# Four-layer cross-attention on one core: layer 2's score products, queries and keys moved between steps, and the mask count cut into eight pieces

## The chip, the core and the metric

The kernel runs on one core of one Trainium2 chip. The metric is device time in microseconds, the median of the runs shown. The core's engines run side by side and wait for each other on semaphores: TensorE (PE) multiplies, VectorE (DVE) does elementwise work and reductions, ScalarE (ACT) does activations and copies out of PSUM, GpSimd (POOL) does elementwise work in SBUF, and SyncE (SP) issues the DMAs. Each engine executes its own instructions in the order written.

## What is computed

Eight batches of 100 rows of width 128 go through four layers with 16 heads of 8. Layers 0, 1 and 3 attend to 1444 rows of context, layer 2 to the first 100 rows of the context under a causal mask, followed by a feed-forward with a GELU.

```
x = L0(x, ctx)        # rmsnorm; 1444 keys; output projection; xn + out
x = L1(x, ctx, mask)  # 1444 keys, score masked to -inf where mask is True; projection; layer norm
x = L2(x, ctx)        # keys = ctx[:, :100] under a causal mask; layer norm;
                      #   gelu(att_h @ W1.T + b1) @ W2.T + b2 + att_h
x = L3(x, ctx)        # 1444 keys; layer norm
```

The mask of layer 1 is an input of booleans and is False everywhere; the kernel counts its non-zero bytes and branches on the count.

## The kernel before

**Units and stages.** A unit is one of the layers 0, 1, 3 for one batch: 24 units. The program is a software pipeline over stages, n = -3 to 24. In stage n, unit n runs its exponentials (`exp`), unit n+1 finishes its running maximum (`top`), unit n+2 projects queries and keys (`prep`), unit n+3 is loaded (`load`), unit n-1 is finished (`post`). Layer 2 of a batch has no stage of its own: its attention (`att2`) rides in the stage four ahead of the batch's layer-3 unit, which makes stages 12 to 19, and its layer norm and feed-forward (`ff2`) in the next, stages 13 to 20.

**Steps.** A stage has 48 steps, `NSTEP = NCH * T`: 12 chunks of 120 or 121 keys by four groups of four heads. In each step PE computes a score tile into one of the three `sexp` banks (`exp_product`), and another, 13 steps ahead (`LEAD`), into one of four `ring` banks (`max_product`). ACT takes exp of the `sexp` tile into `probs` (L1030, `exps`), DVE folds the `ring` tile into the running maximum `mx` (L1246, `maximum`). PE can run three steps ahead of ACT: `exp_product` of step j waits until the exp of step j-3 is done. In every fourth step PE multiplies four steps of `probs` with the values (`values`, L778). `exp_product`, `max_product` and most other products show up at the line of the helper that issues them, L608.

**Where the other work goes.** Three tables of step numbers say behind which step each other piece of work stands, on PE, ACT and DVE alike: `AT` for layers 0, 1 and 3 (xT the transposed input, q the queries, k0 to k2 the keys, v0 to v2 the values, mk0 to mk2 the mask, OT and wo the output projection of `post`, mt0, mt1 and mn the maxima), `AT2` for layer 2's attention (kqv its keys, queries and values; s0 to s3 the scores of four heads each; e0 to e3 their exp on ACT; pt0 to pt3 their transposition), `AT2_FF` for its feed-forward (scale the second half of the layer norm on DVE; at the transposition of its result `att2`; h the hidden layer, whose four GELUs on ACT need another activation table; w2 the second product).

**Who waits for what, near the change.** For a score tile s*t* of layer 2, DVE adds the causal mask (L1327, `causal2`) in the same step and takes the negated maximum (L1333, `maximum2`) in the next, POOL adds it (L525, `less_maximum`), ACT takes exp at e*t* (L1062), PE transposes at pt*t* (L835), ACT copies (L1065). The scores need `kbd2` from POOL (L517, `spread2`). For the queries, PE multiplies at step q, ACT copies to `qh` (L1018), DVE makes `qs` (L1233) in the same step, and POOL spreads it into `qx` (L534). POOL's order in a stage is fixed: context halves (L497, L499), `spread2`, the layer norm's root of `ff2` (L505), `spread`, the root of a layer-1 `post`, four `less_maximum`. The root of `ff2` is what DVE's scale (L1276) waits for.

**Ring banks.** Four `ring` banks serve all products but `sexp` and `acc`. `place` assigns each product a bank in advance, the one planned to be free first, from the step tables and the hold times in `HOLD`; a product waits until the bank's last reader is done.

**The mask count.** In stage -1 (`FLAG_STAGE - 1`), behind v2, ACT adds up all mask bytes, 9025 a partition, in one activation (L1103); at the end of stage 0 PE sums over partitions (L908), ACT writes the flag (L1109), and PE reads it before stage 6.

## Time and profile before

| | us |
|---|---|
| median of 3 runs | 1051.69 (1050.79 to 1053.68) |
| the profiled execution | 1052.03 |
| its span, first to last instruction | 1050.2 |
| PE busy in the span | 947.4 (90%) |
| DVE busy | 839.8 (80%) |
| ACT busy | 717.6 (68%) |
| POOL busy | 372.3 (35%) |

Busy time is the union of an engine's instructions; the rest of the span it waits. TensorE's clock has two levels, 2.4 and 1.2 GHz, and the granted clock is the mean in parts of the higher: 0.958 over the span. At the lower level the same products are busy for about twice as long, so PE's busy time holds both. Stages are told apart by the first `sexp` product of each: stage 0 begins at 76.0 us in the trace, stage 12 at 511.9, stage 20 at 913.4.

### The profile page before, as it was taken

To read this page: it belongs to the slowest core of one execution; us is meant where nothing else is said; L and a number is where in the kernel's file an instruction comes from. 1 tells how busy PE (TensorE), PEld (TensorE's weight loads), DVE (VectorE), ACT (ScalarE), POOL (GpSimd) and SP (SyncE) were. 2 spreads that over 40 slices of the span, in tenths; PEclk is the share of its full clock that TensorE was granted. 3 is DMA by queue.
4 is the path that set the end of the run, shared out by engine and by line. 5 is a ranking of instruction groups with operands and counts; after the bars stand their busy time and mean duration, and the time that the engine had idled before them with its cause. 6 is when DMAs were issued, how large, how long until landed. Compare 5 with 4: busy or idle time off the path is not lost.

```text
span 1050.2 us, 43883 instructions
## 1 busy us (share of the span) xinstructions
PE 947.4 (90%) x18826; PEld 570.9 (54%) x18826; DVE 839.8 (80%) x1804; ACT 717.6 (68%) x1621; POOL 372.3 (35%) x404
## 2 busy tenths in 40 slices
PE   1889999999989999999998979898979898989996
PEld 1346556656656665666564545555645464555552
DVE  7888988889788888889987777777878787869851
ACT  1147777777767777777776676667666676767786
POOL 3835345444323312332543434334343434212100
PEclk9669999999999999999999999999989898999999
DMA  8422313222232233233313121212121211212100
GB/s 225 110 62 72 83 50 88 78 69 60 78 95 69 89 95 104 66 93 96 96 52 86 35 82 38 68 38 69 43 62 44 69 51 61 71 36 66 52 4 6
DMA packets 63641, 73.75 MB, mean 70 GB/s; under 512 B 8130, under 2 KB 59114, under 8 KB 63318
## 3 DMA queue, kind: packets, MB, share of 16 engines
q1 hardware_dynamic: 63446, 70.92, 24.3%
q8 instruction: 150, 2.46, 1.0%
q14 instruction: 45, 0.37, 0.1%
HBM read 50.35 MB, written 18.15 MB: 65 GB/s over the span
## 4 chain that ended last, share of the span: by engine, by line
PE 66%; DVE 20%; ACT 5%; issue 4%; POOL 3%; DMA 1%; SPq 1%; POOLq 0%; ACTq 0%; DVEq 0%
PE ring L608 25%; PE sexp L608 15%; PE acc L778 15%; DVE mx L1246 7%; PE ring L651 6%; DVE mneg L1252 3%; DVE mx L1244 3%; POOL kbd L517 2%; ACT probs L1030 2%; PE ring L835 1%; PE ring L628 1%; DVE kp L1223 1%; PE ring L789 1%; DMA rows<-in_rows 1%; PE ring L734 1%
## 5 line engine op out<-in xcount | busy, mean ns | idle before, releaser
L1246 DVE TENSOR_TENSOR mx<-ring,mx 120x400 f16<-120x400 f32 (+1 forms) x1056 | 564.8, 566 | 114.6 <-PE ring L608 111.7
L1030 ACT ACTIVATE probs<-sexp 120x400 f32<-120x400 f32 (+1 forms) x1152 | 529.9, 509 | 139.2 <-PE sexp L608 134.6
L608 PE MATMUL ring<-qx,krep 96*32 96x400 f16 (+2 forms) x4608 | 418.2, 348 | 30.7 <-DVE mx L1246 8.1
L608 PE MATMUL sexp<-qx,krep 97*32 97x400 f16 (+2 forms) x4608 | 410.9, 340 | 8.4 <-ACT probs L1030 4.2
L778 PE MATMUL acc<-probs,vx 120*18 120x200 f32 (+1 forms) x4608 | 254.6, 336 | 1.0 <-ACT probs L1030 0.7
L608 PEld LDWEIGHTS ring<-qx,krep 96*32 96x32 f16 (+2 forms) x4608 | 133.8, 98 | 130.4 <-DVE mx L1246 42.7
L608 PEld LDWEIGHTS sexp<-qx,krep 97*32 97x32 f16 (+2 forms) x4608 | 133.4, 97 | 94.3 <-ACT probs L1030 28.4
L778 PEld LDWEIGHTS acc<-probs,vx 120*18 120x18 f32 (+1 forms) x4608 | 133.3, 99 | 65.9 <-issue 5.4
L534 POOL TENSOR_TENSOR qx<-qs,headmask 96x400 f16<-96x400 f16 x96 | 78.8, 849 | 150.0 <-DVE qs L1233 150.0
L497 POOL CAST ct<-ctf 128x480 f16<-128x480 f32 (+1 forms) x69 | 40.4, 585 | 135.1 <-PE ring L651 75.0
L608 PE MATMUL ring<-ct,wk 128*32 128x480 f16 (+1 forms) x864 | 65.4, 389 | 20.7 <-DVE mx L1246 20.0
L499 POOL TENSOR_TENSOR ct<-ctf,ct 128x480 f16<-128x480 f32 (+1 forms) x69 | 76.3, 1105 | 5.5
L651 PEld LDWEIGHTS ring<-wv,ct 128*120 128x120 f16 (+1 forms) x864 | 56.4, 139 | 27.5 <-issue 13.7
L651 PE MATMUL ring<-wv,ct 128*120 128x128 f16 (+1 forms) x864 | 66.4, 229 | 2.3 <-DVE kp L1223 1.1
L1244 DVE CAST mx<-ring 121x400 f16<-121x400 f32 x96 | 53.0, 567 | 14.1 <-PE ring L608 14.1
L1000 ACT COPY vx<-ring 120x512 f32<-120x512 f32 (+1 forms) x72 | 42.7, 593 | 28.3 <-PE ring L651 26.9
L990 ACT ACTIVATE kp<-ring,cols 128x480 f16<-128x480 f32 (+1 forms) x48 | 31.7, 661 | 42.3 <-PE ring L608 42.3
L1252 DVE TENSOR_REDUCE mneg<-ring 100x8 f16<-100x968 f16 x48 | 55.5, 1158 | 1.2 <-PE ring L734 1.2
L505 POOL TENSOR_TENSOR rstd<-vare,half 100x1 f32<-100x1 f32 x24 | 13.3, 553 | 116.9 <-DVE vare L1268 116.9
L608 PEld LDWEIGHTS ring<-ct,wk 128*32 128x32 f16 x864 | 27.6, 100 | 37.0 <-issue 25.7
L517 POOL TENSOR_TENSOR kbd<-kq,heads 128x1600 f16<-128x1600 f16 x16 | 45.8, 2880 | 0.6
L1233 DVE SCALAR_TENSOR_TENSOR qs<-qh,headmask,ring 96x400 f16<-96x400 f16 x24 | 15.0, 627 | 36.3 <-ACT qh L1018 36.3
(137 smaller groups left out, 865.0 us busy)
## 6 DMA issues: line engine op xcount, KB each, us to landing
krep<-kept SPq DMA_DIRECT2D x144, 120.0 KB, 2.8
ctf<-in_ctxT SPq DMA_DIRECT2D x16, 722.0 KB
kept<-kp SPq DMA_DIRECT2D x48, 240.0 KB, 3.0
krep<-kept SPq DMA_DIRECT2D x72, 121.0 KB, 2.6
kept<-kp SPq DMA_DIRECT2D x24, 242.0 KB, 2.7
nat<-in_ctx SPq DMA_DIRECT2D x8, 720.0 KB
maskexp<-maskmax SPq DMA_DIRECT2D x8, 281.2 KB, 3.4
anymask<-in_mask SPq DMA_DIRECT2D x1, 1128.1 KB, 10.2
```

The source lines that it names most:

```text
L497: pool.tensor_copy(ct[:, u.par, 0, c0:c0 + n], ctf[:, c0:c0 + n]).then_inc(sem["ct_high"], 1)
L499: pool.tensor_tensor(ct[:, u.par, 1, c0:c0 + n], ctf[:, c0:c0 + n], ct[:, u.par, 0, c0:c0 + n], ALU.subtract).then_inc(sem["ct_low"], 1)
L517: last = pool.tensor_tensor(kbd2[:, i, :, :], kq16[:, i, 0, :].unsqueeze(1).broadcast_to([128, H, S]), heads16[:, :].unsqueeze(2).broadcas ...
L534: last = pool.tensor_tensor(qx[0:PARTS, u.third, t, :, :], qs[:, t, :].unsqueeze(1).broadcast_to([PARTS, HT, S]), headmask16[:, :].unsquee ...
L608: last = run(out[g:g + m], w[:, g:g + m], x, **flags)
L651: last = pe.matmul(ps[0:r, D * i:D * i + D], ct[:, u.par, p, c0:c0 + r], wv16[:, w, u.L, :], start=(j == 0), stop=(j == 2))
L778: last = pe.matmul(acc[32 * q:32 * q + VW, 2 * S * side:2 * S * side + 2 * S], vx[0:r, u.par, PAIRS * c + 2 * t + p, :], probs[0:r, j % PR ...
L1000: act.copy(vx[0:r, u.par, a0:a1, :].rearrange("p a (f e) -> p a f e", f=2)[:, :, :, 0:DH], bank(f"v{g}", u)[0:r, 0:2 * DH * (a1 - a0)].rea ...
L1030: act.activation(probs[0:r, j % PR, :], sexp[j % SR][0:r, 0:QW], ACT.Exp).then_inc(sem["probs_ready"], 1)
L1244: op = dve.tensor_copy(dst, src)
L1246: op = dve.tensor_tensor(dst, src, dst, ALU.max)
L1252: dve.tensor_reduce(mneg[:, 8 * i:8 * i + 8], bank(f"mt{i}", u)[0:S, :].bitcast(F16).rearrange("s (h n) -> s h n", h=8)[:, :, 0:chunk(0)[1 ...
```

## The change

Three things change.

**Step tables.** In every stage xT goes from step 18 to 13 and q from 20 to 16; k1 from 22 to 24, v0 from 24 to 25, v1 from 27 to 28, k2 from 30 to 31, mk0 to mk2 one step later each. In layer 2's attention the scores go from steps 23, 25, 26, 28 to 20, 21, 22, 23, their exp from 29, 31, 32, 34 to 26, 27, 29, 30, their transposition from 32, 34, 35, 38 to 27, 29, 30, 32, and the last three pieces two steps earlier. In the feed-forward, scale and at go one step later (13 and 17), h stays at 19, and w2 goes from 27 to 34.

**Mask count.** Eight activations of 1129 bytes a partition (the last of 1122) in stage 0, behind steps 4, 9, ..., 39, instead of one of 9025 in stage -1.

**Flag.** PE sums eight columns instead of one, and ACT adds these up in one more activation, on which its own copy waits.

```diff
-AT = {"ct0": 0, "ct1": 3, "ct2": 6, "O": 7, "k0": 10, "OT": 12, "wo": 15, "xT": 18, "q": 20, "k1": 22, "v0": 24,
-      "mk0": 25, "v1": 27, "mk1": 28, "k2": 30, "mk2": 31, "v2": 33, "power": 25, "scale": 32, "mt0": 36, "mt1": 37, "mn": 41}
+AT = {"ct0": 0, "ct1": 3, "ct2": 6, "O": 7, "k0": 10, "OT": 12, "xT": 13, "wo": 15, "q": 16, "k1": 24, "v0": 25,
+      "mk0": 26, "v1": 28, "mk1": 29, "k2": 31, "mk2": 32, "v2": 33, "power": 25, "scale": 32, "mt0": 36, "mt1": 37, "mn": 41}
...
-AT2_FF = {"out": 0, "scale": 12, "at": 16, "h": 19, "w2": 27}
+AT2_FF = {"out": 0, "scale": 13, "at": 17, "h": 19, "w2": 34}
...
-        maskcount = sb("maskcount", [128, 1])
+        maskcount = sb("maskcount", [128, 8])
+        masksum = sb("masksum", [1, 9])
...
-                pe.matmul(ps[0:1, 0:1], maskcount[:, :], ones[:, :], start=True, stop=True
+                pe.matmul(ps[0:1, 0:8], ones[:, :], maskcount[:, :], start=True, stop=True
...
-                    if n == FLAG_STAGE - 1 and j == AT["v2"] + 1:
+                    if n == FLAG_STAGE and j % 5 == 4 and j < 40:
                         act.wait_ge(sem["mask_in_all"], 16)
-                        act.activation(anymask[:, :], anymask[:, :], ACT.Copy, accum_out=maskcount[:, :]
+                        piece = anymask[:, j // 5 * 1129:min(j // 5 * 1129 + 1129, B * S * KEYS // 128)]
+                        act.activation(piece, piece, ACT.Copy, accum_out=maskcount[:, j // 5:j // 5 + 1]
                                        ).then_inc(sem["mask_counted"], 1)
...
-                        act.copy(maskflag[:, :], bank("flag", None)[0:1, 0:1]).then_inc(sem["flag_ready"], 1)
+                        act.activation(masksum[:, 0:8], bank("flag", None)[0:1, 0:8], ACT.Copy, accum_out=masksum[:, 8:9]
+                                       ).then_inc(sem["flag_summed"], 1)
+                        act.wait_ge(sem["flag_summed"], 1)
+                        act.copy(maskflag[:, :], masksum[:, 8:9]).then_inc(sem["flag_ready"], 1)
```

How PE's instructions stand behind the hidden layer (`aT2,w1`, step 19) in stage 14, before; steps 20 to 22, the queries behind step 20 and the keys k1 behind step 22:

```order
L608 MATMUL ring1<-aT2,w1 32x100 x16
L608 MATMUL sexp2<-qx,krep 32x400 x4
L608 MATMUL ring0<-qx,krep 32x400 x4
L608 MATMUL ring2<-which16,bq16 32x400 x3
L608 MATMUL ring2<-xT,wq 32x100 x12
L608 MATMUL sexp0<-qx,krep 32x400 x4
L608 MATMUL ring3<-qx,krep 32x400 x4
L608 MATMUL sexp1<-qx,krep 32x400 x4
L608 MATMUL ring0<-qx,krep 32x400 x4
L778 MATMUL acc<-probs,vx 18x200 x8
L608 MATMUL ring3<-ct,wk16 32x480 x12
```

And now, to the third score tile (`kbd2,kq16`, of whose six rows each the first stands):

```order
L609 MATMUL ring0<-aT2,w1 32x100 x16
L609 MATMUL sexp2<-qx,krep 32x400 x4
L609 MATMUL ring2<-qx,krep 32x400 x4
L609 MATMUL ring1<-kbd2,kq16 32x400 x3
...
L609 MATMUL sexp0<-qx,krep 32x400 x4
L609 MATMUL ring3<-qx,krep 32x400 x4
L609 MATMUL ring2<-kbd2,kq16 32x400 x3
...
L609 MATMUL sexp1<-qx,krep 32x400 x4
L609 MATMUL ring1<-qx,krep 32x400 x4
L779 MATMUL acc<-probs,vx 18x200 x8
L609 MATMUL ring3<-kbd2,kq16 32x400 x3
```

Three score tiles stand where the queries and k1 stood; the fourth follows behind step 23 and k1 behind step 24.

DVE's instructions in the same stretch before, with the queries' `qs` behind the maximum of step 20:

```order
L1246 TENSOR_TENSOR mx<-ring0,mx 120x400
L1265 ISA squared,mv<-xn 100x128
L1265 ISA mv 100x1
L1233 SCALAR_TENSOR_TENSOR qs<-qh,headmask,ring2 96x400
L1246 TENSOR_TENSOR mx<-ring3,mx 120x400
L1268 TENSOR_SCALAR vare<-mv 100x1
L1246 TENSOR_TENSOR mx<-ring0,mx 120x400
L1246 TENSOR_TENSOR mx<-ring2,mx 120x400
```

And now:

```order
L1251 TENSOR_TENSOR mx<-ring2,mx 120x400
L1270 ISA squared,mv<-xn 100x128
L1270 ISA mv 100x1
L1332 TENSOR_TENSOR sc2<-ring1,causal 100x400
L1251 TENSOR_TENSOR mx<-ring3,mx 120x400
L1273 TENSOR_SCALAR vare<-mv 100x1
L1338 TENSOR_REDUCE max2<-sc2 100x4
L1332 TENSOR_TENSOR sc2<-ring2,causal 100x400
L1251 TENSOR_TENSOR mx<-ring1,mx 120x400
L1338 TENSOR_REDUCE max2<-sc2 100x4
```

`qs` stands four steps further ahead, and two instructions for each score tile stand between the maxima of steps 20 to 24.

ACT's instructions early in stage 0 now, with the first piece of the mask count behind step 4:

```order
L979 ACTIVATE ctf<-ring3,cols 128x480
L1031 ACTIVATE probs<-sexp1 121x400
L1105 ACTIVATE anymask,maskcount<-anymask 128x1129
L1031 ACTIVATE probs<-sexp2 121x400
L1031 ACTIVATE probs<-sexp0 121x400
```

Seven more such pieces follow; before, no such row stood in stage 0.

## Rows read from the trace of the kernel before

**Rows 1.** Stretches: length; busy PE, PEld, DVE, ACT, POOL; clock, DMA share, GB/s.
```profile
76.00:113.20 37.20, 36.15 (x693) 22.17 (x697) 30.45 (x58) 26.29 (x59) 16.75 (x16) 0.94 0.27 73
...
511.90:553.90 42.00, 40.80 (x860) 25.52 (x852) 36.24 (x80) 31.39 (x75) 20.34 (x22) 1.00 0.27 76
...
607.00:657.40 50.40, 44.62 (x916) 27.26 (x908) 38.55 (x92) 34.35 (x79) 19.28 (x20) 0.97 0.22 61
657.40:709.20 51.80, 46.17 (x920) 28.38 (x912) 38.70 (x93) 34.51 (x79) 19.28 (x20) 0.93 0.19 54
...
553.90:955.00 401.10, 355.46 (x7100) 217.15 (x7096) 307.78 (x715) 271.64 (x618) 146.54 (x155) 0.94 0.20 57
```

**Rows 2.** Stages 13 to 20 grouped: line, engine, operation, count; busy, mean ns; idle before, releasers.
```profile
L608 PE MATMUL ring<-qx,krep 96*32 96x400 f16 (+2 forms) x1540 | 141.4, 347 | 15.0 <-DVE mx L1246 5.5 <-DVE kp L1223 5.1 <-DVE y L1363 2.9
L608 PE MATMUL ring<-ct,wk 128*32 128x480 f16 (+1 forms) x288 | 20.8, 389 | 19.8 <-DVE mx L1246 19.8
...
L608 PE MATMUL ring<-ident,att 100*32 100x100 f32 x64 | 3.7, 313 | 5.2 <-DVE att L1280 3.5 <-DVE mx L1246 1.7
```

**Rows 3.** PE in stage 14: start, us, instruction, idle before and its releaser.
```profile
619.97 0.35 PE L608 MATMUL ring<-qx,krep 96*32 96x400 f16 x4 [1.21 <-DVE mx L1246]
...
623.19 0.86 PE L608 MATMUL ring<-aT,w 128*32 128x100 f32 x32
...
629.64 0.84 PE L608 MATMUL ring<-ct,wk 128*32 128x480 f16 x12 [2.79 <-DVE mx L1246]
...
634.85 0.34 PE L608 MATMUL sexp<-qx,krep 97*32 97x400 f16 x4
...
635.19 0.85 PE L778 MATMUL acc<-probs,vx 120*18 120x200 f32 x16
635.87 0.68 PE L608 MATMUL ring<-kbd,kq 128*32 128x400 f16 x12
636.38 0.34 PE L608 MATMUL sexp<-qx,krep 97*32 97x400 f16 x4
```

**Rows 4.** ACT in stage 14 around the GELUs.
```profile
623.82 1.28 ACT L1076 ACT_TABLE_LOAD   x1
625.11 1.05 ACT L1076 ACTIVATE hT<-ring,cols 128x100 f32<-128x100 f32 x4
626.18 1.28 ACT L1030 ACT_TABLE_LOAD   x1
627.47 0.50 ACT L1030 ACTIVATE probs<-sexp 120x400 f32<-120x400 f32 x1
```

**Rows 5.** DVE in stage 14: the scale, the queries, and one score tile.
```profile
619.08 0.35 DVE L1276 SCALAR_TENSOR_TENSOR xn<-xn,rstd,rows 100x128 f32<-100x128 f32 x1 [1.66 <-POOL rstd L505]
...
628.38 0.62 DVE L1233 SCALAR_TENSOR_TENSOR qs<-qh,headmask,ring 96x400 f16<-96x400 f16 x1 [3.16 <-ACT qh L1018]
...
635.07 0.57 DVE L1327 TENSOR_TENSOR sc<-ring,causal 100x400 f32<-100x400 f32 x1
...
636.04 0.56 DVE L1333 TENSOR_REDUCE max<-sc 100x4 f32<-100x400 f32 x1
```

**Rows 6.** POOL in stage 14.
```profile
612.82 5.72 POOL L517 TENSOR_TENSOR kbd<-kq,heads 128x1600 f16<-128x1600 f16 x2
```

**Rows 7.** The stretch of stage 14 behind the GELUs, columns as in rows 1.
```profile
630.00:633.80 3.80, 3.80 (x51) 2.31 (x40) 2.65 (x6) 1.56 (x3) 2.94 (x5) 0.55 0.05 16
```

**Rows 8.** Two fp32 additions on DVE in stages 2 and 17.
```profile
165.64 0.71 DVE L1319 TENSOR_TENSOR xall<-y,xall 100x128 f32<-100x128 f32 x1
...
768.81 2.45 DVE L1309 TENSOR_TENSOR y<-y,xall 100x128 f32<-100x128 f32 x1
```

**Rows 9.** The mask count and the start of stage 0, all engines.
```profile
66.15 7.73 ACT L1103 ACTIVATE anymask<-anymask 128x9025 uint8<-128x9025 uint8 x1
...
71.70 0.29 PE L742 MATMUL ring<-ident,mneg 100*16 100x100 f16 x1
...
73.87 0.21 ACT L1023 COPY mrow<-ring 16x100 f16<-16x100 f16 x1
```

More of the change, by code:

```diff
@@ L904, in flag_sum @@
             def flag_sum():
[L906 removed]
+                pe.wait_ge(sem["mask_counted"], 8)
                 ps = begin("flag", None)
[L908 removed]
+                pe.matmul(ps[0:1, 0:8], ones[:, :], maskcount[:, :], start=True, stop=True
                           ).then_inc(sem["flag_filled"], 1)
```

7 lines of the change are left out of this document (3 added, 4 removed).

## The prediction, made before the changed kernel was run

> **What bounds the kernel now.** I read the stretches by stage first, then the grouped waits of stages 13 to 20, then that part of stage 14 engine by engine.
>
> The reader is to see that the kernel has two regimes [rows 1]. In a stage without the feed-forward PE is the bound: stage 12, with layer 2's attention alone, has PE busy 40.80 of 42.00 us at full clock. In stages 13 to 20 it is not: stage 14 takes 50.40 us with PE busy 44.62, stage 15 51.80 with 46.17, while DVE is busy 38.6 and ACT 34.4 in both. So no engine is full there; instructions wait for each other in turn, and the clock is lower: 0.94 over the 401.1 us of these eight stages.
>
> Two waits of PE make most of it [rows 2]. Before the keys' product (`ring<-ct,wk`) PE idles 19.8 us in these stages, 2.79 in stage 14 [rows 3]. Before the maximum's products it idles 10.6 for `mx` and `kp` together, before the feed-forward's transposition 5.2.
>
> The first of them is the GELU. ACT loads the GELU's table at 623.82, does four GELUs, loads exp's table again and is back at exp at 627.47 [rows 4]: 3.65 us without an exp. PE can go three steps on. But in those steps stands the queries' product, DVE waits for its copy `qh`, which ACT makes only behind the next exp: 3.16 us [rows 5]. Meanwhile the ring banks stay full, and PE stops before k1, until 629.64, although exp ran again 2.2 us earlier. Right behind that the clock is down: 0.55 from 630.0 to 633.8 [rows 7].
>
> The second is the layer norm's root. POOL makes `kbd` until 618.54 [rows 6], its root comes behind that, DVE's scale at step 12 waits 1.66 us for it until 619.08 [rows 5], and PE waits 1.21 us for DVE's maxima [rows 3] and again before the transposition.
>
> **The sum is made against the profiled execution, 1052.0 us** (span 1050.2 and 1.8 around it), which is 0.3 above the median shown.
>
> **The GELU wait.** Let H be the end of the issue of the hidden layer's products, 624.05 in stage 14 (0.86 long from 623.19 [rows 3]). Exp is back at H+3.4, its first tile done at H+3.9, and step 23's `sexp` needs that one. What stands in steps 20 to 22 now: three steps at 0.34 (634.85 to 635.19 [rows 3]), one values product at 0.68 (635.19 to 635.87), three score tiles at 0.51 (635.87 to 636.38): 3.23 us in a hole of 3.9. DVE has none of its work waiting for ACT any more; per step it has a maximum, an addition of the mask and a reduction, 0.57, 0.57 and 0.56, which follow each other about 0.5 apart (635.07 and 636.04 hold two starts with a maximum between [rows 5]), so 1.5 us a step against PE's 0.85 to 1.5. Followed bank by bank through the four rings (the hidden layer keeps one of them until the GELUs are done) it is never more than four products behind until k1, which finds its bank free some 0.3 us late. PE's wait becomes 0.7 + 0.3 = 1.0 instead of 2.8. Stage 20 has no scores (no `att2`), so its hole is filled by 1.7 us only and about 2.2 remain. Eight stages: 19.8 before, 7 x 1.05 + 2.2 = 9.6 after. **-10.2 us.** Bounds: nothing left gives -19.8; DVE keeping PE as long as now gives 0.
>
> **The root's wait.** The scale moves one step later, behind one more maximum, so DVE waits 1.1 instead of 1.7 us, and the bank that PE waits for has been freed before the wait. PE also brings two pieces forward over the place where it stalls: xT, and q, together about 1.4 us of products that stood behind it. In stages 13 to 16 (1.21 us in stage 14, and some 0.4 of the 1.7 that `mx` has in the 5.2) I leave 0.4 each. In 17 to 19 DVE is late for another reason, an addition of 0.28 us that takes 2.45 [rows 8] while POOL makes `kbd`; that stays where it is, but the 1.4 us of PE work still shorten PE's stop, from 2.7 (5.1 for `kp` and most of the 3.5 for `att`, in three stages) to 1.45. Stage 20's half a microsecond goes. Of 15.8 us (5.5 + 5.1 + 5.2 [rows 2]) some 6 to 7 remain. **-9.0 us**, between -4 (only xT covers) and -15.8.
>
> **The clock.** Of stages 14 and 15, with the same work, 15 has more time at 1.2 GHz (0.93 against 0.97) and is 1.40 us longer [rows 1]. 0.94 over 401.1 us is about (1 - 0.94) x 2 x 401 = 48 us at 1.2 GHz; the difference of 14 and 15, 3.6 to 4.2 us at that level for 1.4, prices it at 0.35 a us, 16 to 17 us together. The stretches at 1.2 GHz follow the two waits: 630.0 to 633.8 comes right behind the 2.79 us. With waits of 1.0 and 0.4 us in their place I expect them to go from most stages, and to stay in stage 20 and in two or three places of 17 to 19. **-14.0 us**, between -3 and -17. This is the largest term and the least certain: the trace has no wait of 1.0 us in the middle of such a stretch to read the outcome from. Stage 12, where PE idles 1.2 us in all, keeps the full clock.
>
> **What the moved scores cost later.** exp and transposition of a tile stand one or two steps apart instead of three. ACT needs 0.5 for the step's exp and about 0.5 for the tile's, PE has 0.9 to 1.6 us of its own between, so the four transpositions meet their data within about 0.1 us: 28 of them with the GELU and 4 in stage 12, **+2.8**. Bounds: 0, and 32 x 1.0 = 32 if nothing covers them. In stage 12 no hole exists; the four tiles in consecutive steps put 7.2 us of DVE work beside 5 to 6 of PE: **+0.7**, between 0 and 2. w2, seven steps later, takes its DVE wait of 2.9 us in all [rows 2] with it: 0. The earlier xT and q and the later keys in the stages without layer 2 only change places among PE's products while PE is full: 0, give or take 0.05 us in each of 15 stages. k1's copies reach SP later by two steps, and the replicated keys are used some twenty steps after that, so SP hides it.
>
> **The mask count.** The activation of 7.73 us ends at 73.88 and the copy of the maxima, which stage 0's first exp product needs, stands behind it at 73.87, while PE had the row ready at 71.99 [rows 9]: **-1.8**. In stage 0 ACT is busy 26.29 of 37.20 us, PE 36.15 [rows 1]. A piece takes 7.73/8 = 0.97 plus a fixed part; the fixed part of an ACTIVATE isn't shown apart, bounded by 0 and the whole 0.50 of an exp, I take 0.2: eight pieces 9.3 us, which makes ACT 35.6 busy. It is nearly as full as PE, and each piece delays three or four exps by up to 1.2 us where PE's lead over ACT is three short steps: 0.25 a piece, **+2.0**, between 0 and 6. The longer flag chain ends stages before its reader: 0.
>
> **Sum:** 1052.0 - 10.2 - 9.0 - 14.0 + 2.8 + 0.7 - 1.8 + 2.0 = **1022.5 us**.
>
> **Rivals.**
> *The clock doesn't come back.* Shorter waits still bring the 1.2 GHz stretches in most stages. Only 3 us of the 14 come: 1033.5. For it: stage 15 has the same waits as stage 14 and more time at 1.2 GHz (0.93 against 0.97 [rows 1]), so a second, shorter wait than the GELU's can be enough. Against: in stage 14 it was not.
>
> *Everything fits.* No wait above 0.5 us is left but stage 20's: the terms above with -15, -12, -16.5 and +1.0 for the rest: 1009.5. Against it is DVE, which gets its eight extra instructions in five steps.
>
> *VectorE and GpSimd hold each other.* A fp32 addition in SBUF on DVE took 0.71 us [rows 8] and 2.45 when POOL was in an instruction, where it takes 0.28 alone. q's spreading on POOL (four instructions of 0.85) moves from steps 21 to 25 to steps 17 to 20, where such additions of a layer-0 or layer-1 `post` stand, and w2's second addition moves to step 36, where POOL makes the next context. Up to 0.4 us for the first in 16 stages and 0.6 for the second in 8: 11 us if all is on the path; half of it gives 1028. The page "SBUF — State Buffer", section "Terms", of the Trainium skill says of the shared port pair that it is held for the full instruction and the loser blocks fully; rows 8 agree.
>
> *Slower: ACT becomes the gate of the transpositions.* If POOL's subtraction of a maximum comes later than ACT's step 26, exp of tile 0 waits, all exps behind it wait, and PE stands before pt0 to pt3 with one step of its own work. Each costs the unhidden chain of 1.0 us or more, 32 times, and the clock stays low besides: 1052.0 - 10.2 - 9.0 - 3 + 32 + 0.9 = 1062.7. It decides at POOL being 3.5 us late: the tile's maximum is there at about H+3.4, POOL's 0.85 later, ACT's step 26 at H+8.
>
> *The scores can't start that early.* They need `kbd`, ready 11.5 us into stage 14 [rows 6]; step 20 comes behind the hidden layer's products at 16.2 [rows 3]. Nothing speaks for it.
>
> **Chances.** Forecast 0.55; the clock doesn't come back 0.17; everything fits 0.10; the shared hold 0.10; gate of the transpositions 0.05; something else that eats it all, near no change, 0.03. The predicted time is the forecast's, 1022.5. The range reaches from 1009 to 1039: the low end is "everything fits", the high end is the low clock kept together with half of the hold or a dearer stage 0 (1033.5 + 5.5); what lies outside is the slower rival, no change, and tails. About 0.3%, 3 us, is what a measurement of this kernel can tell from none. Faster by more than that 0.92, within it 0.04, slower 0.04.
>
> **What the profile after would show.** Stages 13 to 19 at 46.5 to 48 us instead of 50.4 to 53, stage 20 near 39.5; granted clock 0.98 or more over the span. PE's longest wait in stage 14 before step 23's `sexp` or step 24's k1, 0.5 to 1 us, its releaser ACT's exp or DVE's maximum; DVE's `qs` waiting under 0.6. Stage 0 beginning at 74.2 and 39 us long. I am wrong if PE still waits over 2 us behind the hidden layer, if the transpositions (L836) show waits above 0.3 us each, or if the clock of stages 13 to 19 stays at 0.93 to 0.97 with short waits.

## The result, and the profile of the changed kernel

The changed kernel takes 1045.45 us, median of 5 runs (1042.32 to 1047.78), against 1052.52 us for the kernel before, median of 5 runs beside it: a ratio of 0.9927, 95% interval 0.9906 to 0.9947. It is faster, by 7.1 us where 29.5 were forecast, and the time lies outside the range of 1009 to 1039.

The profiled execution took 1042.32 us, with a span of 1040.5 against 1050.2. The time of each stage shows where it came from. A stage is counted here from ACT's first exp of it to that of the next, which for stage 0 is 0.6 us behind the first `sexp` product; the last row ends with the last instruction:

| stages | before, us | after, us | difference | forecast |
|---|---|---|---|---|
| ahead of stage 0 | 76.66 | 74.01 | -2.7 | -1.8 |
| 0 | 37.11 | 39.27 | +2.2 | +2.0 |
| 1 to 4 | 148.5 | 146.6 | -1.9 | 0 |
| 5 to 8 | 144.6 | 147.9 | +3.3 | 0 |
| 9 to 11 | 105.6 | 110.5 | +4.8 | 0 |
| 12 | 41.92 | 45.73 | +3.8 | +1.1 |
| 13 to 20 | 401.2 | 382.5 | -18.7 | -30.8 |
| 21 to 23 | 94.7 | 94.2 | -0.5 | 0 |

(The 2.8 us for transpositions are divided here as 2.45 in stages 13 to 20 and 0.35 in stage 12.)

The stretches, columns as in [rows 1]: stage 0, stage 10, stage 12, stages 14 and 15, stages 17 and 18, and stages 13 to 20 together.

```profile
74.00:113.30 39.30, 37.82 (x700) 21.32 (x696) 32.28 (x61) 34.88 (x80) 16.72 (x16) 0.91 0.25 65
443.90:480.96 37.06, 35.00 (x736) 20.86 (x728) 32.94 (x70) 27.41 (x63) 10.55 (x14) 1.00 0.29 85
517.70:563.40 45.70, 41.66 (x853) 24.67 (x848) 36.84 (x80) 31.81 (x75) 20.50 (x22) 1.00 0.25 70
612.56:660.18 47.62, 43.55 (x915) 25.79 (x906) 39.90 (x93) 34.58 (x80) 19.72 (x20) 1.00 0.23 65
660.18:707.29 47.11, 43.39 (x909) 26.00 (x913) 39.09 (x91) 34.13 (x79) 19.58 (x20) 1.00 0.21 59
756.15:803.50 47.35, 42.23 (x896) 25.42 (x892) 40.71 (x91) 33.86 (x78) 19.73 (x20) 1.00 0.21 59
803.50:854.85 51.35, 46.14 (x898) 27.71 (x893) 41.06 (x91) 34.27 (x78) 19.72 (x20) 0.90 0.19 55
563.40:945.85 382.45, 346.23 (x7101) 207.02 (x7096) 314.83 (x714) 270.32 (x618) 149.03 (x155) 0.97 0.21 60
```

Stage 14 went from 50.40 to 47.6 and stage 15 from 51.80 to 47.1, as forecast; stages 13, 16, 18 and 19 lie above the 46.5 to 48 that were forecast, at 49.2, 48.9, 51.4 and 51.3. PE is idle for 382.45 - 346.23 = 36.2 us in the eight stages where it was idle for 401.10 - 355.46 = 45.6. So half of the gain, 9.4 us, is less waiting. The other half, 9.2, is less busy time for the same products, nearly all of it the clock: 23.9 us at 1.2 GHz in place of 44.4. Stage 18 has the clock at 0.90 and is 4.0 us longer than stage 17, though both wait 5.1 to 5.2 us. And stages 9 to 12, which have no feed-forward, lost their tight packing: in stage 10 PE idles 2.1 us, where it idles 0.76 in the same stage with the old steps (below).

PE's waits of stages 13 to 20, columns as in [rows 2]:

```profile
L609 PE MATMUL sexp<-qx,krep 97*32 97x400 f16 (+1 forms) x1537 | 140.3, 342 | 4.4 <-ACT probs L1031 4.2 <-DMA qx<-mrow 0.2
L609 PE MATMUL ring<-qx,krep 96*32 96x400 f16 (+1 forms) x1540 | 139.0, 341 | 13.4 <-DVE kp L1228 7.3 <-DVE mx L1249 5.4
...
L609 PE MATMUL ring<-kbd,kq 128*32 128x400 f16 (+1 forms) x336 | 19.3, 333 | 2.3 <-DVE mx L1251 1.9
L609 PE MATMUL ring<-ct,wk 128*32 128x480 f16 (+1 forms) x288 | 18.9, 367 | 0.9 <-DVE mx L1251 0.9
L836 PE MATMUL ring<-ident,sc 100*100 100x100 f32 x112 | 15.4, 260 | 1.0 <-ACT sc L1063 0.7
...
L846 PE MATMUL ring<-pT,v 100*18 100x200 f32 x112 | 6.3, 341 | 6.6 <-DVE mx L1249 6.6
L609 PE MATMUL ring<-ident,xall 100*32 100x100 f32 x120 | 5.5, 254 | 3.1 <-DVE mx L1251 1.5 <-DVE kp L1228 1.5
...
L609 PE MATMUL ring<-which,bq 36*32 36x400 f16 x24 | 3.1, 380 | 2.9 <-DVE mx L1251 2.9
```

The 36.2 us are four groups, against the same four before:

- the GELU's: 4.4 + 2.3 + 0.9 = 7.6, before 19.8;
- steps 12 to 16, where DVE waits for the root and `kbd` holds its additions: 7.3 + 3.1 + 2.9 = 13.3, before 15.8;
- the end of the stage, from step 28 on: 5.4 + 6.6 = 12.0, before 2.9 for `y` and 3.8 ahead of the output's transposition, 6.7;
- all others: 3.3, before 3.3.

The third group was not in the prediction. It grew by 5.3 us.

Stage 14 on PE: the hidden layer, the hole of the GELU, and the end of the stage.

```profile
628.91 0.87 PE L609 MATMUL ring<-aT,w 128*32 128x100 f32 x32
...
631.47 0.69 PE L609 MATMUL ring<-kbd,kq 128*32 128x400 f16 x12 [0.49 <-DVE mx L1251]
...
635.85 0.79 PE L609 MATMUL ring<-ct,wk 128*32 128x480 f16 x12 [0.22 <-DVE mx L1251]
...
652.99 0.35 PE L609 MATMUL ring<-qx,krep 96*32 96x400 f16 x4 [0.60 <-DVE mx L1249]
...
654.63 0.87 PE L846 MATMUL ring<-pT,v 100*18 100x200 f32 x16 [0.95 <-DVE mx L1249]
```

The 2.79 us before k1 [rows 3] are now 0.49 before a score tile and 0.22 before k1: the scores fill the hole as worked out. The two waits at steps 39 and 40 are new. Step 36 of the same stage on DVE shows what stands ahead of them:

```profile
650.39 1.15 DVE L1257 TENSOR_REDUCE mneg<-ring 100x8 f16<-100x968 f16 x1
651.47 0.98 DVE L1372 TENSOR_TENSOR xall<-y,att 100x128 f32<-100x128 f32 x1
652.38 0.56 DVE L1249 CAST mx<-ring 121x400 f16<-121x400 f32 x1
652.86 1.15 DVE L1257 TENSOR_REDUCE mneg<-ring 100x8 f16<-100x968 f16 x1
```

and on POOL at the same time:

```profile
650.54 0.58 POOL L498 CAST ct<-ctf 128x480 f16<-128x480 f32 x1
651.20 1.10 POOL L500 TENSOR_TENSOR ct<-ctf,ct 128x480 f16<-128x480 f32 x1
```

`xall<-y,att` is w2's second addition. The 34 in `AT2_FF` brought it to step 36, between two reductions of 1.15 us and beside POOL's next context. It takes 0.98 us there and 0.28 where POOL is not in the way. It ends at 652.45, POOL's instruction at 652.30.

### The profile page after: what moved, and what is told of

Its sections match the earlier page's. It is cut to its first block, busy times and chain, and to the rows that moved or that the text cites. A ratio compares the mean times of both kernels' runs of the same rounds, so it can differ in the third digit from the quotient of the medians.

```text
span 1040.5 us, 43899 instructions
## 1 busy us (share of the span) xinstructions
PE 940.1 (90%) x18826; PEld 554.9 (53%) x18826; DVE 852.9 (82%) x1804; ACT 721.5 (69%) x1637; POOL 376.2 (36%) x404
## 4 chain that ended last, share of the span: by engine, by line
PE 60%; DVE 26%; ACT 5%; issue 4%; POOL 3%; DMA 2%; SPq 1%; POOLq 0%; ACTq 0%; DVEq 0%
PE ring L609 23%; PE sexp L609 13%; PE acc L779 13%; DVE mx L1251 7%; PE ring L652 5%; DVE mneg L1257 5%; DVE mx L1249 4%; POOL kbd L518 2%; PE ring L836 1%; PE ring L629 1%; ACT probs L1031 1%; DMA qx<-mrow 1%; DVE qs L1238 1%; PE ring L790 1%; DMA rows<-in_rows 1%
## 5 line engine op out<-in xcount | busy, mean ns | idle before, releaser
L609 PE MATMUL ring<-qx,krep 96*32 96x400 f16 (+2 forms) x4608 | 415.0, 346 | 30.7 <-DVE mx L1249 13.3
L609 PEld LDWEIGHTS ring<-qx,krep 96*32 96x32 f16 (+2 forms) x4608 | 129.7, 98 | 126.3 <-DVE mx L1251 36.2
L652 PEld LDWEIGHTS ring<-wv,ct 128*120 128x120 f16 (+1 forms) x864 | 54.8, 136 | 26.8 <-DVE mx L1251 11.9
L609 PE MATMUL ring<-ct,wk 128*32 128x480 f16 (+1 forms) x864 | 60.0, 383 | 4.1 <-DVE mx L1251 2.9
L506 POOL TENSOR_TENSOR rstd<-vare,half 100x1 f32<-100x1 f32 x24 | 13.3, 556 | 131.7 <-DVE vare L1273 131.7
L513 POOL CAST kq<-k 128x200 f16<-128x200 f32 x8 | 2.8, 352 | 96.1 <-ACT v L1054 96.1
L545 POOL CAST maskb<-mask 100x480 bf16<-100x480 uint8 (+1 forms) x24 | 13.4, 597 | 62.4 <-DMA mask<-in_mask 62.4
```

The costliest lines, as they stand in the source:

```text
L609: last = run(out[g:g + m], w[:, g:g + m], x, **flags)
L652: last = pe.matmul(ps[0:r, D * i:D * i + D], ct[:, u.par, p, c0:c0 + r], wv16[:, w, u.L, :], start=(j == 0), stop=(j == 2))
```

## Experiments

Every experiment is timed against runs of the kernel before that stand beside it, 1051.71 to 1053.31 us at the median. "The changed kernel" is the one of the diff, 1045.45 us. It was not timed again beside the experiments. Where one of them is compared with it, the difference is one of two medians from different sets of runs; its own runs reach from 1042.3 to 1047.8, so such a difference is good to some 3 us, and the stage times of the profiles stand beside it. Its parts come first, then each place that had lost time, then combinations.

### The mask count alone

The kernel before with `maskcount`, `masksum` and the eight pieces of the change, and its tables as they were:

```diff
-                    if n == FLAG_STAGE - 1 and j == AT["v2"] + 1:
+                    if n == FLAG_STAGE and j % 5 == 4 and j < 40:
```

> The kernel before with the mask count's edit alone; the three step tables stay as before. Theory A (what the two traces show stage by stage): stage 0 begins 2.6 us earlier and is 2.2 us longer, everything else alike, so 1052.0 +- 1, no change. Rival B: the flag chain or the pieces also shift the clock's phase or stage 1 (which was 1.2 us shorter in the changed kernel), so this edit alone is worth 1.5 us or more: 1050.5 or less.

Measured: 1052.18 us, 10 runs, ratio 0.9996 (0.9984 to 1.0007). No change. Stage 0 begins at 74.01 instead of 76.66, and is 40.75 us long instead of 37.11: what is won ahead of it is given back in it. Part of that is the clock: stage 0 has 9.3 us at 1.2 GHz here, 6.9 in the changed kernel and 4.1 before. In the changed kernel the first piece and the instruction that reads its sum out are, on ACT:

```profile
79.32 1.15 ACT L1105 ACTIVATE anymask<-anymask 128x1129 uint8<-128x1129 uint8 x1
80.35 0.20 ACT L1105 ACTIVATION_READ_ACCUMULATOR anymask<-anymask 128x1 f32 x1
80.45 0.90 ACT L1031 ACTIVATE probs<-sexp 121x400 f32<-121x400 f32 x2
```

The rows overlap: the next exp starts 1.13 us behind the piece, the read-out included, where I took 0.97 + 0.2. ACT's busy time in stage 0 says the same, 34.88 instead of 26.29 us, 1.07 a piece.

### Each half of the tables alone

`AT` alone (queries and xT ahead of the GELU, keys behind it) on the kernel before:

```diff
-AT = {..., "wo": 15, "xT": 18, "q": 20, "k1": 22, "v0": 24, ...}
+AT = {..., "xT": 13, "wo": 15, "q": 16, "k1": 24, "v0": 25, ...}
```

> The kernel before with the new table AT alone (xT, q earlier; keys, values, mask one or two steps later). Theory A: the 1.4 to 1.9 us that stages 9 to 11 lost and the 0.45 of stages 7 and 8 come from this table, through VectorE's additions held by GpSimd's earlier spreading and through the bank that xT waits for; so these stages are as long as in the changed kernel (35.6, 35.6, 36.7, 37.0, 36.75), and in stages 13 to 19 VectorE's qs no longer waits 3.2 us for ScalarE. Without scores in the GELU's hole PE waits about 2.2 us before step 23's exp product instead of 2.8 before k1. Time 1049 +- 3. Rival B: the losses of stages 9 to 12 come from layer 2's tables; then stages 7 to 11 are as before, and the time is 1044 or less.

Measured: 1049.73 us, 10 runs, ratio 0.998 (0.9967 to 0.9993). PE's wait after the hidden layer is now for ACT's exp itself, in stage 14 of this kernel:

```profile
634.99 0.35 PE L608 MATMUL sexp<-qx,krep 97*32 97x400 f16 x4 [1.96 <-ACT probs L1030]
```

So with the queries out of the hole what is left of 2.8 us is 2.0. Ahead of the hidden layer PE waits 0.37 us before xT at step 13 and then before the output projection at step 15:

```profile
626.59 0.42 PE L608 MATMUL ring<-wo,oT 128*32 128x128 f32 x8 [1.22 <-DVE mx L1246]
```

That is 1.59 us in two stops, where before it was 1.21 + 0.43 = 1.64: the pieces brought forward did not shorten this stop. Stages 13 to 20 give 12.3 us, and stages 5 to 12 take 11.6 of them back: they are 40.1, 37.2, 35.6, 35.6, 36.7, 37.2, 36.7 and 44.7 us here, already nearly what the changed kernel has. The loss of stages 5 to 12 is `AT`'s.

`AT2` and `AT2_FF` alone (the scores in the hole, the queries still in it):

```diff
-AT2 = {"cx": 2, "kqv": 5, "s0": 23, "s1": 25, "s2": 26, "s3": 28, "e0": 29, ..., "a": 42, "o": 44, "out": 45}
-AT2_FF = {"out": 0, "scale": 12, "at": 16, "h": 19, "w2": 27}
+AT2 = {"cx": 2, "kqv": 5, "s0": 20, "s1": 21, "s2": 22, "s3": 23, "e0": 26, ..., "a": 40, "o": 42, "out": 43}
+AT2_FF = {"out": 0, "scale": 13, "at": 17, "h": 19, "w2": 34}
```

> The kernel before with the new tables of layer 2 alone (AT2, AT2_FF). The queries stay at step 20, so VectorE still waits for ScalarE's copy behind the GELUs, and the three score tiles queue behind that. Theory A: GELU's wait stays above 2 us in stages 13 to 19, the tail (values2 at step 40 behind the reductions of the maxima) costs 1.0 us in each of stages 12 to 19, stages 0 to 11 as before: 1054 +- 4. Rival B: filling the hole with scores is what helps, with or without the queries: 1042 or less.

Measured: 1064.02 us, ratio 1.0115 (1.0086 to 1.0144). It is slower, by 11 us, more than either expectation had. In its stage 17 PE waits before a score tile:

```profile
785.95 0.69 PE L608 MATMUL ring<-kbd,kq 128*32 128x400 f16 x12 [3.10 <-DVE sc L1327]
```

The score tile needs a bank, DVE should free it, and DVE stands in front of `qh` as in [rows 5]. Scores put behind a waiting DVE only move PE's stop. The two halves give -3.0 and +11.3 us alone and -7.1 together (the mask count alone changes nothing): the order of the queries is the condition for the scores, and neither half can be priced without the other.

### Layer 2's end two steps later again

The changed kernel, with the end of layer 2's attention at its old steps:

```diff
-       "pt0": 27, "pt1": 29, "pt2": 30, "pt3": 32, "a": 40, "o": 42, "out": 43}
+       "pt0": 27, "pt1": 29, "pt2": 30, "pt3": 32, "a": 42, "o": 44, "out": 45}
```

> The changed kernel with layer 2's last pieces back where they were (values product 42, transposition 44, its reading 45, instead of 40, 42, 43). Theory A: in the changed kernel PE waits 0.6 us at step 39 and 0.95 us at step 40 for VectorE, which is behind with the two reductions of 1.16 us each at steps 36 and 37; two steps later VectorE has caught up, the 0.95 goes and 0.55 before the transposition comes back as it was: 0.5 to 1 us a stage in 8 stages, and the 1.2 GHz stretches at 45 us into stages 16, 18, 19 go: 1036 to 1041. Rival B: VectorE is the bound there, and the wait only moves to the next ring bank: no change, 1045.

Measured: 1039.28 us (1034.00 to 1044.11, 4 runs), ratio 0.9864 (0.9818 to 0.991). In stage 14 PE idles 3.91 us, and 4.07 in the changed kernel: the waits moved, to 0.61 and 0.68 before the maximum's products and 0.54 before the output's transposition. The stage is 47.6 us in both. So the place of the values product is not the cause. What gain there is comes in stages 16 and 18, which happen to have no time at 1.2 GHz in this profile, the runs scatter by 10 us, and the interval touches that of the changed kernel. How much of it is the edit's I leave open.

### POOL's spreading of the queries

The changed kernel leaves out three of the four `qx` multiplications in layers 1 and 3, so those layers read old queries; only the time is of interest:

```diff
-                for t in range(T):
+                for t in range(T if u.L == 0 else 1):
                     last = pool.tensor_tensor(qx[0:PARTS, u.third, t, :, :],
```

> The changed kernel, with GpSimd leaving out three of the four multiplications that spread the queries of layers 1 and 3 (so it leaves part of the computation out; layer 0 is whole). GpSimd is then busy 0.85 us instead of 3.3 behind VectorE's qs in stages 6 to 20. Theory A, the hold: VectorE's y addition (0.74 us in the changed kernel, 0.28 before), xn (0.59) and squared (0.45) in stages 9 to 12 come back to 0.28, and those stages lose at least 0.6 us of the 1.4 to 1.9 that they had gained. Rival B, bank order: the durations come back but PE waits for the same banks, and stages 9 to 11 stay within 0.2 us of 36.7 to 37.0.

Measured: 1041.67 us in a single run. To see what it tests, first the changed kernel's stage 11, DVE and POOL:

```profile
495.17 0.74 DVE L1327 TENSOR_TENSOR y<-y,xall 100x128 f32<-100x128 f32 x1
...
496.32 0.27 DVE L1265 TENSOR_REDUCE mv<-y 100x1 f32<-100x128 f32 x1
...
496.99 0.59 DVE L1267 SCALAR_TENSOR_TENSOR xn<-mv,y 100x128 f32<-100x128 f32 x1
...
497.99 0.46 DVE L1270 CUSTOM_DVE_ANT_0 squared<-xn 100x128 f32<-100x128 f32 x1
```

```profile
494.92 3.38 POOL L535 TENSOR_TENSOR qx<-qs,headmask 96x400 f16<-96x400 f16 x4 [6.44 <-DVE qs L1238]
```

Three small DVE instructions take 0.74, 0.59 and 0.46 us there, and 0.28 each before the change, when POOL's spreading stood elsewhere. With the shorter spreading the second and third are back at 0.28, and stages 9 to 12 are 35.8, 36.3, 36.3 and 45.2 us instead of 36.7, 37.0, 36.8 and 45.7. That is 2.6 of the 8.6 us that these four stages had lost. The first addition still takes 0.74 in stages 10 to 12, beside the one multiplication that is left, so it is a lower bound for this hold. The hold is not all: PE's wait of 0.37 us at step 13 stands ahead of the spreading and is unchanged.

### xT one step later

```diff
-AT = {..., "OT": 12, "xT": 13, "wo": 15, ...}
+AT = {..., "OT": 12, "xT": 14, "wo": 15, ...}
```

> The changed kernel with the transposed input at step 14 instead of 13. In the changed kernel PE waits at step 13 for the bank whose last reader is VectorE's key split (0.37 us in stages 7 to 16, 0.5 in 17 to 19, where 2.4 us more follow). Theory A: this wait is the planned bank's, so at step 14 it is gone or below 0.1, and stages 7 and 8 go from 35.6 to 35.2. Rival B: PE is simply ahead of VectorE there, and the wait comes back one product later: stages 7 and 8 within 0.1 of 35.6.

Measured: 1040.06 us in a single run. The wait of 0.37 us for xT's ring bank at step 13 is gone, and stages 7 and 8 are 0.3 us shorter, at 35.3. In stage 14 PE stops 1.04 us at step 16 instead of 0.37 and 0.66 at steps 13 and 16. The row in stage 14:

```profile
624.03 0.35 PE L609 MATMUL ring<-qx,krep 96*32 96x400 f16 x4 [1.04 <-DVE mx L1251]
```

So beside a feed-forward the stop is as long as before and only stands at one place. Whether the kernel as a whole is faster than the changed one a single run does not settle.

### The new steps only beside a feed-forward

The changed kernel with `AT` and `AT2` chosen by stage: the old ones wherever there is no feed-forward (`AT_OLD` and `AT2_OLD` hold the old numbers).

```diff
+                self.AT, self.AT2 = (AT, AT2) if self.ff2 is not None else (AT_OLD, AT2_OLD)
...
-                    if s.prep is not None and j == AT["q"]:
+                    if s.prep is not None and j == s.AT["q"]:
                         queries(s.prep)
```

> The changed kernel, but with the new step tables only in the stages that hold the feed-forward (13 to 20); in all others, 12 among them, the tables of before. Theory A: the 9 us that stages 5 to 12 lost come from the new tables there and are given back but for the first low-clock stretch of stage 6, stages 13 to 20 stay as in the changed kernel within the clock's luck: 1034 to 1039. Rival B: what a stage's table costs or saves is owed by the next stage, so that the sum is about as now: 1043 or more.

Measured: 1034.59 us, ratio 0.9837 (0.9813 to 0.9861). Its stages 10 and 12:

```profile
442.68:477.85 35.17, 34.41 (x739) 21.02 (x734) 31.71 (x69) 26.94 (x62) 10.47 (x14) 1.00 0.31 89
513.16:555.10 41.94, 40.73 (x853) 25.56 (x848) 36.18 (x80) 31.42 (x75) 20.37 (x22) 1.00 0.26 76
```

They are back at 35.17 and 41.94 us, stage 14 stays as it was, and the whole is 10.9 us faster than the changed kernel between the medians (7.8 between the profiled executions; stage 0 is 1.8 longer here). In the profile stages 5 to 12 are 10.5 us shorter. So moving pieces in stages in which hardly anything waited cost 10.5 to 11 us, where I had put 0 (and 0.7 for stage 12).

### Layer 3's additions behind `kbd`

In stages 17 to 19 one addition still stood beside `kbd`, as in [rows 8]. In the changed kernel's stage 17, DVE:

```profile
764.11 0.99 DVE L1311 TENSOR_TENSOR y<-oatt,rows 100x128 f32<-100x128 f32 x1
765.02 0.56 DVE L1251 TENSOR_TENSOR mx<-ring,mx 120x400 f16<-120x400 f32 x1
765.50 2.45 DVE L1314 TENSOR_TENSOR y<-y,xall 100x128 f32<-100x128 f32 x1
767.88 0.71 DVE L1228 SCALAR_TENSOR_TENSOR kp<-ring,cols,kp 128x484 f16<-128x484 f32 x1
```

and POOL:

```profile
762.09 5.72 POOL L518 TENSOR_TENSOR kbd<-kq,heads 128x1600 f16<-128x1600 f16 x2
```

`kbd` is two instructions of 2.86 us. The first ends near 764.95, and the addition that started in it ends at 765.10; the second ends at 767.81 and the next addition at 767.95. The edit moves two parts of `output` of layer 3 and the first half of its norm three steps later, past `kbd`:

```diff
-                            if j == AT["O"] + 1 + part:
+                            if j == AT["O"] + 1 + part + 3 * (u.L == 3 and part > 1):
                                 output(u, part)
-                            if u.L == 3 and j == AT["O"] + 5 + part:
+                            if u.L == 3 and j == AT["O"] + 8 + part:
                                 centre(u, y[:, 0, :], "own_o", part)
```

> The changed kernel with layer 3's last additions (bias and residual) and its layer norm's first half three steps later, behind GpSimd's kbd. In stages 17 to 19 one addition takes 2.46 us where it takes 0.28 alone, and PE waits 2.37 us before step 14's maximum. Theory A: that addition's hold is the whole wait and also what takes the clock down at 11 us into stages 18 and 19; with it gone PE waits under 0.8 there, and stages 17 to 19 take 45.5 to 47.5 us instead of 47.4, 51.4, 51.3: 1033 to 1040. Rival B: VectorE then waits for the root of the feed-forward's norm instead (1.1 us as in stages 14 to 16) and the clock falls in about as many places: less than 3 us gained, 1042 or more.

Measured: 1035.14 us, ratio 0.9827 (0.9799 to 0.9855), 10.3 us faster than the changed kernel (7.1 between the profiled executions). The wait of 2.37 us in stages 17 to 19 is gone, and they are 45.95, 47.61 and 47.60 us instead of 47.35, 51.35 and 51.28, with 6.8 us at 1.2 GHz together instead of 20.4.

### w2 four steps earlier

```diff
-AT2_FF = {"out": 0, "scale": 13, "at": 17, "h": 19, "w2": 34}
+AT2_FF = {"out": 0, "scale": 13, "at": 17, "h": 19, "w2": 30}
```

> The changed kernel with w2 at step 30 instead of 34. There, VectorE's second addition behind w2 takes 1.0 us (0.28 before), held by GpSimd's context halves, right ahead of the two reductions of 1.16 us, and PE waits 0.6 and 0.95 us at steps 39 and 40. Theory A: the hold and the crowd are the tail's waits; with w2 four steps earlier the addition takes 0.28 again and the two waits fall by 0.7 us or more together in each of stages 13 to 20: 1038 to 1042. Rival B: the reductions alone make the waits; the addition gets short and the waits stay within 0.2 us: no change from 1045.

Measured: 1029.48 us (1029.29 to 1030.28), ratio 0.9782 (0.9767 to 0.9798). This one number is worth 16.0 us between the medians and 13.0 between the profiled executions, more than either expectation had. In its stage 14, DVE and then PE:

```profile
646.50 0.28 DVE L1372 TENSOR_TENSOR xall<-y,att 100x128 f32<-100x128 f32 x1
```

```profile
652.70 0.87 PE L846 MATMUL ring<-pT,v 100*18 100x200 f32 x16 [0.62 <-DVE mx L1249]
```

The addition takes 0.28 us, the two waits of 0.60 and 0.95 are one of 0.62, and stage 14 is 46.30 us instead of 47.57.

To see whether it is the product's place or the addition's, the next one leaves w2 at step 34 and moves only the second addition, from step 36 to 43:

```diff
-                        if j == AT2_FF["w2"] + 1 + part:
+                        if j == AT2_FF["w2"] + 1 + 8 * part:
```

> The changed kernel with w2 left at step 34, but VectorE's second addition behind it eight steps later (step 43 instead of 36), when GpSimd has finished the context halves. The product, its place on TensorE and its reading at step 35 stay. Theory A, the hold: the addition took 1.0 us at step 36, between the two reductions, and made the tail's waits; away from there it takes 0.28, stages 14 and 15 get 0.6 to 1.2 us shorter and the 1.2 GHz stretches of stages 16, 18, 19 thin out as with w2 at 30: 1028 to 1035. Rival B, the crowd: it is w2's 1.07 us product and its reading at steps 34 and 35 that put TensorE and VectorE behind; then less than 0.4 us a stage is gained and the time is 1040 or more.

Measured: 1031.70 us (1030.62 to 1032.07), ratio 0.98 (0.9782 to 0.9818). This gives 13.8 of the 16.0 us (10.3 of 13.0 between the profiled executions), and one wait of 0.83 us stands at step 40. So it is the addition that stood in the wrong place. Of its 0.98 us there 0.70 is hold; both runs move the whole of it, so what the other 0.28 between the reductions costs is not told apart.

### POOL's root ahead of `kbd`

The prediction's root term rests on POOL's order. This edit turns it round in the changed kernel:

```diff
+                if s.ff2 is not None:
+                    root(s.ff2)
                 if s.att2 is not None:
                     spread2(s.att2)
-                if s.ff2 is not None:
-                    root(s.ff2)
```

> The changed kernel with GpSimd's root of the feed-forward's norm put ahead of its making of kbd. VectorE's scale waits for it 1.2 us in stages 13 to 16 of the changed kernel, where the prediction left PE a wait of 0.4 and PE waits 0.65 to 0.95 at step 16 and 0.37 at step 13. Theory A: the 0.65 is the root's; with the root at 6 us into the stage the scale waits 0, PE's wait at step 16 goes below 0.2, stages 13 to 16 get 0.5 to 1.0 us shorter each; but kbd ends 1.5 us later, and in stages 17 to 19 it holds VectorE's residual addition longer (2.4 to 4 us): 1040 to 1048 in all. Rival B: PE's wait at step 16 is VectorE's own load and stays above 0.5.

Measured: 1060.09 us (1057.37 to 1061.09), ratio 1.0066 (1.0042 to 1.009): slower, by 14.6 us against the changed kernel, and 12 above the expectation's upper end. Stage 14 of this kernel, POOL, then DVE, then PE:

```profile
619.78 0.55 POOL L506 TENSOR_TENSOR rstd<-vare,half 100x1 f32<-100x1 f32 x1 [13.58 <-DVE vare L1273]
...
621.36 5.72 POOL L518 TENSOR_TENSOR kbd<-kq,heads 128x1600 f16<-128x1600 f16 x2
```

```profile
621.66 2.70 DVE L1308 TENSOR_TENSOR oatt<-oatt,rows 100x128 f32<-100x128 f32 x1
```

```profile
624.42 0.38 PE L609 MATMUL ring<-ident,oatt 100*32 100x100 f32 x8 [2.00 <-DVE oatt L1308]
```

The root is early now, DVE no longer waits for it (1.19 us in the changed kernel's stage 14). But `kbd` starts 1.7 us later against DVE's program, and `oatt<-oatt,rows` falls 0.3 us into its first half instead of 2.0 us into it. It takes 2.70 us instead of 0.98, and PE stops 2.00 us for it. Stages 14 to 16 are 51.1 us long, with 6.8 us each at 1.2 GHz. PE's wait of 0.66 us at step 16 is gone, so that one was the root's; its wait at step 12 has grown from 0.28 to 2.00. DVE's wait for the root had been cheaper than what replaced it.

### Combinations

The choice of steps by stage together with layer 3's additions three steps later:

> The changed kernel with the new tables only in the feed-forward's stages and layer 3's last additions three steps later, nothing else. Each alone gave 1034.6 and 1035.1 against 1045.5 for the changed kernel. If the two are independent, as their stages are, the sum is 1024 to 1029; if the clock's luck is shared, 1031 or more.

Measured: 1025.91 us, ratio 0.974 (0.9722 to 0.9759). Together they give 19.5 us, apart 10.9 + 10.3.

All four, with xT at step 14 and w2 at step 30:

> A version meant to beat both: the changed kernel with the new tables only in the feed-forward's stages, layer 3's last additions three steps later, the transposed input at step 14 instead of 13, and w2 at step 30 instead of 34 (so that its second addition stands ahead of GpSimd's context halves). If the mechanisms add up: stages 5 to 12 as before (-9 from the changed kernel's profile), stages 17 to 19 without the 2.4 us wait and its low clock (-7), w2 without the hold (0 to -5): 1025 to 1033. If they share one slack: 1033 or more.

Measured: 1016.22 us (1015.61 to 1017.74, 5 runs), ratio 0.9656 (0.9642 to 0.967), the fastest kernel of this study: 37 us below the kernel before, 29 below the changed one, and 9 below the lower end of what I had expected. Its stage 14:

```profile
603.10:649.50 46.40, 43.27 (x916) 25.97 (x908) 39.01 (x92) 34.46 (x79) 19.57 (x20) 1.00 0.23 66
```

Stages 5 to 12 take 293.8 us, near the 292.1 before the change and not the 304.1 after it, stages 13 to 20 take 363.9 us instead of 382.5, and from stage 0 on there are 19.0 us at 1.2 GHz, against 38.1 after the change and 51.9 before.

The same kernel with the mask counted as before the change:

> The version meant to beat both (e9), but with the mask counted as before, in one activation in stage -1. Counting in pieces alone changed nothing against before (1052.2 against 1052.7). Theory A: here too the two counts are equal within 1.5 us of each other, since the 2.6 us gained ahead of stage 0 are paid back in it. Rival B: the pieces pay back less now or then: the old count is 2 us or more slower.

Measured: 1018.79 us, ratio 0.9672 (0.9654 to 0.969), against 0.9656 (0.9642 to 0.967) with the pieces. The intervals overlap: what the pieces are worth here isn't settled.

And with POOL's root ahead of `kbd`:

> The fastest version so far (e9) with the root ahead of kbd as well. There the residual addition of layer 3 stands at step 13 to 14 behind kbd. Theory A: the root's wait is the last large one ahead of the GELU (1.0 us at step 16 in stages 14 to 16, 1.85 in 17 to 19); without it these stages get 0.7 us shorter or more and the time is 1008 to 1013. Rival B: kbd, ending 1.5 us later, holds an addition again and gives it back: 1015 or more.

Measured: 1029.70 us, ratio 0.9782 (0.976 to 0.9803), 13.5 us slower than with the root behind. PE stops 2.00 us before `ring<-ident,oatt` at step 12 here too. Having cleared the other places does not help: the price of the exchange is about the same in both kernels.

## Why the prediction was wrong

**The bound and the GELU wait: right.** The hole was read rightly and the scores fill it. 19.8 us became 7.6, where 9.6 were forecast. Stage 20's remainder is 2.18 us where 2.2 were worked out. In stage 14 the forecast had 0.7 before step 23's exp product and 0.3 at k1. Measured are no wait at the first and 0.22 at the second, and 0.49 for a bank at the second score tile; in stages 17 to 19 step 23 has 0.63 to 0.74. That the queries have to go ahead is shown by the two halves of the tables.

**The root's wait: -2.5 us instead of -9.0.** The failed step is "the 1.4 us of PE work still shorten PE's stop". xT and q can't fill the stop, because they need ring banks, which the late DVE has to free. Two runs show it: with `AT` alone the stop is 0.37 + 1.22 us instead of 1.21 + 0.43, and with xT one step later 0.37 + 0.66 become 1.04. So PE now stops before xT (3.1 us) and before q (2.9 us), and in stages 17 to 19 still 2.37 us at step 14 (the addition of 2.45 us in [rows 8]). In stages 13 to 16 of the changed kernel, where DVE's scale also stands a step later, it is 0.37 + 0.66 or so instead of 1.21 + 0.43; in 17 to 19 it is 0.52 + 2.37 where it was 1.69 + 0.99, so nothing was won there. The bound that I gave, -4 for "only xT covers", did not reach far enough. That the additions beside `kbd` make the wait of 2.37 us in stages 17 to 19 is shown by moving them.

**w2, "seven steps later": 5.3 us more waiting instead of 0.** The failed step is "takes its DVE wait of 2.9 us with it: 0". I had costed the product and its wait. I had left the two additions behind it to a rival, at 0.6 us in eight stages, of which half were on the path. The hold is 0.7 us, but it stands between reductions of 1.15 us at the one place where PE's banks are tight, and two waits of 0.6 and 0.95 us came of it. Moving the addition gives 10 to 16 us, against 5.5 us of hold in the eight stages together. In stages 13 to 20 PE's idle time falls by 6.7 us with w2 at 30 and by 6.3 with the addition alone moved; the rest there is PE's busy time, with 10.2 and 17.1 us at 1.2 GHz instead of 23.9.

**"The earlier xT and q only change places": +8.1 us in stages 5 to 11 instead of 0, and +3.8 in stage 12 instead of +1.1.** The failed step is "only change places among PE's products while PE is full". It does matter: DVE is at 32.9 of 37.1 us and has little to give, the bank for xT comes 0.37 us late, k1 waits 0.61 in stage 11, and POOL's spreading holds three of DVE's instructions. In stage 12 PE's waits grew from 1.2 to 4.0 us, of which 1.3 are at the scores and k1 between steps 21 and 24, 0.71 at the first transposition and 0.63 at the values product. The choice of steps by stage gives 10.5 of these 11.9 us back; of what stays 1.2 us are in stage 6, where 3.4 us at 1.2 GHz remain. The shorter spreading gives 2.6 of the 11.9. The remaining 6 us of stages 9 to 12 are for the most part waits for banks at several places, which I did not tell apart.

**The clock: -8 to -9 instead of -14.** Stages 13 to 20 have 23.9 us at 1.2 GHz instead of 44.4 (the prediction had 48, from the rounded clock); the difference, at 4.0 us for the 10.2 us that separate stages 17 and 18, is 20.5 x 0.39 = 8.0 us. PE's busy time, which falls by 9.2, says about the same. The price was about right (0.35), the amount was not: 3.4 us in stage 16 and 10.2 in each of stages 18 and 19 are left. Take two stretches of 6.8 us at the same 2.37 us wait, which ends at 768.65 in stage 17 and at 816.00 in stage 18:

```profile
767.30:774.10 6.80, 5.45 (x140) 3.39 (x144) 6.73 (x18) 2.91 (x8) 2.91 (x5) 1.00 0.29 77
...
814.80:821.60 6.80, 5.60 (x77) 3.25 (x81) 4.86 (x14) 1.43 (x4) 1.47 (x3) 0.50 0.32 94
```

The granted clock is 1.00 (2.4 GHz) and 0.50 (1.2 GHz). A wait of that length decides nothing by itself, and why one stage is spared and the next not stays open. Besides, 3.4 us at 1.2 GHz came new in stage 6.

**The transpositions: less than +2.8** (32 of them at 0.1 would have been 3.2). One of the four waits, 0.71 us in stages 12 and 13; nearly all others meet their data. **The mask: right in sum** (-2.65 and +2.16 in the profile, no change by itself), and the piece was, with 1.13 us for the 1.17 forecast. Of the +2.16, by 0.39 a us, some 1.1 belong to the 2.8 us more at 1.2 GHz in stage 0, an estimate, so the pieces' own delay is nearer 1 us than the 2.0 forecast.

**The rivals.** The hold of VectorE by GpSimd was the mechanism of the miss at the end of the stage and of a part of that in stages 9 to 12; it had a chance of 0.10 and a price of 5.5 us. The instructions it names, w2's second addition and those beside the spreading, cost 10 to 16 and at least 2.6 us. "The clock doesn't come back" happened by half. Of the slower rival, ACT as the gate of the transpositions, nothing is seen but the 0.71 us named above. Against the profiled run the forecast was 19.8 us short: 6.5 at the root, 5.3 at the end of the stage, 4.8 at the clock (by PE's busy time), 8.2 up to stage 12, less 2.0 at the GELU and 3.0 at the transpositions and elsewhere. The run itself lies 3.1 us below the median.

## What to carry to other kernels

Look through every instruction that a moved step issues on DVE for those with two operands in SBUF, and lay POOL's timeline beside their new place: what is left of POOL's instruction is what they take. A piece moved forward over a stall fills it only if it has its own bank; if it takes one of those that the late engine frees, it only brings the stall forward. And give a table of steps to the stages that need it: a stage in which hardly anything waits has little to win from a new order.
